# Cross-attention and self-attention in one block of instructions, with self-attention's buffers on memory that cross-attention has finished with

## The reference

```
def xattn(x, context, Wq, Wkv, null_kv, Wout, ln_scale, ln_bias):     # 16 heads of 64
    q = split_heads(x @ Wq) * 64 ** -0.5
    k, v = split(context @ Wkv)                       # a null key and value stand ahead of each
    out = softmax(q @ k.T) @ v                        # 256 x 512 for each batch and head
    return layernorm(out @ Wout) * ln_scale + ln_bias

def ffn(x, ...):                                      # 16 query heads of 8, 8 key heads
    h = rmsnorm(x) * ln1_w
    q, k, v = rope(h @ wq), rope(h @ wk), h @ wv
    x = x + softmax(causal(q @ k.T / sqrt(8))) @ v @ wo
    h = rmsnorm(x) * ln2_w
    return x + moe(h)                                 # softmax router, 2 of 8 experts

x = x + xattn(layernorm(x), ctx_2048, ...)
x = x + ffn(layernorm(x), ...)
```

## Time and profile before

| | us |
|---|---|
| median of 3 executions | 651.12 (650.49 to 651.89) |
| the profiled execution | 651.96 |
| its span, first to last instruction | 649.9 |
| busy PE, DVE, ACT, POOL in the span | 567.8, 495.3, 419.7, 322.9 |

### The profile page before, as it was taken

One profiled execution on the slowest core, in us unless ns is written; L12 is line 12 of the kernel. 1 busy time (PEld: TensorE's weight loads), 2 busy tenths in 40 slices (PEclk: granted clock), 3 DMA queues, 4 the chain that ended last, 5 costly groups with the idle time before them and its releaser, 6 DMA issues. The chain is left out here.

```text
span 649.9 us, 11036 instructions
## 1 busy us (share of the span) xinstructions
PE 567.8 (87%) x3380; PEld 444.1 (68%) x3380; DVE 495.3 (76%) x1030; ACT 419.7 (65%) x1024; POOL 322.9 (50%) x606
## 2 busy tenths in 40 slices
PE   2959999999999889999987748899986599999996
PEld 1737868777677677787766636665554578888885
DVE  4757877886889587888689625998984479999995
ACT  2538777786767657777667415898883365656653
POOL 1345766785678765787667646466965100000000
PEclk9989999999999899999989865999998599999999
DMA  7020000000100000000000002002220000000001
GB/s 263 2 59 1 2 33 2 1 2 2 32 2 2 2 1 1 1 2 2 2 0 2 2 21 73 1 3 86 85 86 2 0 1 1 1 1 1 2 0 33
DMA packets 14393, 13.14 MB, mean 20 GB/s; under 512 B 2048, under 2 KB 13696, under 8 KB 14336
## 3 DMA queue, kind: packets, MB, share of 16 engines
q1 hardware_dynamic: 14032, 12.41, 6.0%
q10 hardware_dynamic: 304, 0.03, 0.0%
HBM read 11.92 MB, written 0.52 MB: 19 GB/s over the span
## 5 line engine op out<-in xcount | busy, mean ns | idle before, releaser
L1071 POOL TENSOR_SCALAR attn_probs<-attn_probs,rinv 128x512 f32<-128x512 f32 x128 | 87.4, 695 | 29.5 <-DVE rinv L975 29.5
L848 ACT ACTIVATE attn_probs<-bank,bias 128x512 f32<-128x512 f32 x128 | 87.3, 687 | 10.0 <-DVE bias L968 10.0
L984 DVE TENSOR_TENSOR pT_lo<-bank,pT_hi 128x512 fp32r<-128x512 f32 x128 | 87.4, 685 | 7.2 <-ACT pT_hi L864 5.8
L701 PE MATMUL bank<-ident,attn_probs 128*128 128x128 f32 x512 | 77.6, 285 | 12.5 <-POOL attn_probs L1071 11.8
L960 DVE TENSOR_REDUCE neg_max<-bank 128x1 f32<-128x512 f32 x128 | 82.0, 682 | 6.7 <-PE bank L686 6.7
L864 ACT ACTIVATE pT_hi<-bank 128x512 fp32r<-128x512 f32 x128 | 73.3, 594 | 15.3 <-PE bank L701 15.0
L701 PEld LDWEIGHTS bank<-ident,attn_probs 128*128 128x128 f32 x512 | 57.4, 143 | 36.5 <-POOL attn_probs L1071 21.0
L731 PE MATMUL bank<-pT_hi,vals 128*128 128x256 f32 x256 | 67.6, 295 | 2.2 <-DVE pT_lo L984 1.4
L731 PE MATMUL bank<-pT_lo,vals 128*128 128x256 f32 x256 | 65.6, 288 | 0.0
L1885 ACT ACTIVATE act_hi<-act_f 128x512 fp32r<-128x512 f32 x56 | 35.4, 633 | 43.4 <-DVE act_f L1926 43.3
L731 PEld LDWEIGHTS bank<-pT_hi,vals 128*128 128x128 f32 x256 | 49.9, 195 | 4.3 <-issue 1.7
(11 more groups left out here) (311 smaller groups left out, 1614.5 us busy)
## 6 DMA issues: line engine op xcount, KB each, us to landing
ctx_raw<-in_ctx SPq DMA_DIRECT2D x4, 512.0 KB, 4.8
wkv_raw<-in_L_xattn_Wkv SPq DMA_DIRECT2D x2, 1024.0 KB, 10.4
gu_raw<-in_L_ffn_w_gate SPq DMA_DIRECT2D x4, 448.0 KB, 3.6
gu_raw<-in_L_ffn_w_up SPq DMA_DIRECT2D x4, 448.0 KB, 4.4
dn_raw<-in_L_ffn_w_down SPq DMA_DIRECT2D x4, 448.0 KB, 5.4
x<-in_x SPq DMA_DIRECT2D x1, 512.0 KB, 6.8
wq_raw<-in_L_xattn_Wq SPq DMA_DIRECT2D x1, 512.0 KB, 10.3
wout_raw<-in_L_xattn_Wout SPq DMA_DIRECT2D x1, 512.0 KB, 12.1
```

Source lines behind the costliest of these rows:

```text
L701: last = pe.transpose(t_bank[half][:, j * N + t * P:j * N + (t + 1) * P], probs[:, g % 2, i, t, kt * P:(kt + 1) * P], k.ident[:, :])
L848: act.activation(probs[:, g % 2, i, t, :], score_bank(G, i)[:, :], ACT.Exp, bias=bias[:, t, h:h + 1], scale=X_SCALE, accum_out=row_sum[:, ...
L984: dve.tensor_tensor(pT_lo[:, i, 2 * half:2 * half + 2, :], t_bank[half][:, :].rearrange("p (j n) -> p j n", j=2), f(pT_hi[:, i, 2 * half:2 ...
L1071: pool.tensor_scalar(probs[:, g % 2, i, t, :], probs[:, g % 2, i, t, :], rinv[:, t, h:h + 1], 1.0, ALU.mult, ALU.mult).then_inc(p_norm_s, 1)
```

## The change

Both attentions become one block, in one function `attention`, which calls `self_attention` as a supplier of pieces. The buffers of self-attention are laid over memory of cross-attention in such an order that those used first lie on what is done first (the projection weights); what cross-attention keeps to the end lies under the experts' weights. PE's banks are the same memory as before.

- Batch 0's quads are all made by POOL, ahead of its step 29; batch 1's ahead of step 32; clearing and the values of batches 0 and 1 ahead of step 33; the rest of POOL's list comes after step 34.
- PE makes the four `features` of batch 0 at the ends of steps 29 to 32; ACT copies the first two in steps 29 and 30 (with the constants in 29), DVE the others in 31 and 32.
- Self-attention's steps -3 and -2 stand at the ends of steps 32 and 33, its steps -1 and 0 at the start of step 34, ahead of the last output projection; its steps 1 and later follow step 34.
- Batch 3's steps become 1 ("y"), 6 ("h") and 8 ("qkv"); DVE takes the moments of y in step 2, the residual in 3, `make_h` in 5, the rotation in 10.

```
     S.units_done = (k_ps, NP - AHEAD), (v_ps, NP - AHEAD), (v_lo_s, NP - AHEAD)
     S.queries_done, S.scored, S.exps_done = (q_lo_s, NP), (p_exp, 4 * NP), (t_lo_s, 4 * NP)
     S.weighted = o_ps, 2 * NP
...
# PE (ACT and DVE alike, with their own steps of first_features)
+            later = S.tensor(pe)
             for s in STEPS:
+                if s == NP + 2:
+                    later.step(-1)
+                    later.step(0)
                 transpose_probs(s - 1, 1, 1)
...
                 context_unit(s, 1)
+                if NP - 3 <= s < NP + 1:
+                    later.first_features(s - NP + 3)
+                if NP <= s + 0 < NP + 2 and s > NP - 1:
+                    later.step(s - NP - 3)
+            for s in range(1, later.END):
+                later.step(s)
...
# POOL
+            later = S.gpsimd(pool)
             for s in STEPS:
+                if s == NP - 3:
+                    later.quads(0)
+                if s == NP:
+                    later.quads(1)
+                if s == NP + 1:
+                    later.first_values()
                 whole_sum(s, 1)
...
+            later.rest()
...
-        POST_STEPS = {-3: "y", 5: "h", 7: "qkv"}
+        Y_STEP, H_STEP, QKV_STEP = 1, 6, 8
+        POST_STEPS = {Y_STEP: "y", H_STEP: "h", QKV_STEP: "qkv"}
...
+            def quads(b):
+                if b == 0:
+                    for done in S.units_done:
+                        pool.wait_ge(*done)
+                query_quads(b)
+                key_quads(b)
+
+            def first_values():
+                pool.wait_ge(*S.weighted)
+                pool.memset(oT[:, :, :], 0.0).then_inc(zero_s, 1)
+                pool.memset(f(v_all[:, :, :, 2 * HD]), 1.0)
+                values(0, 2)
+
+            def rest():
+                values(2, LATE_BATCH)
+                scale_y(pool, k, LATE_BATCH)
+                quads(2)
+                scale_x1(pool, k, LATE_BATCH)
+                scale_h(pool, k, LATE_BATCH)
+                split_hT(pool, k, LATE_BATCH)
+                attention_out(0)
+                rotate_keys(pool, k, LATE_BATCH)
+                values(LATE_BATCH, B)
+                quads(3)
+                attention_out(1)
...
             def extra(s):
-                if s == -3:
+                if s == Y_STEP:
                     turn_y(pe, k, LATE_BATCH, free_bank("y", LATE_BATCH))
-                if s == 5:
+                if s == H_STEP:
                     turn_h(pe, k, LATE_BATCH, free_bank("h", LATE_BATCH))
-                if s == 7:
+                if s == QKV_STEP:
                     project_qkv(pe, k, LATE_BATCH, free_bank("qkv", LATE_BATCH))
...
-            for a in (0, 2):
-                last = act.activation(query_slot(0, a), query_heads(0), ACT.Copy, scale=F_SCALE)
```

More of the change, by code:

```diff
@@ L509, in split_hT, with attention @@
     pool.tensor_tensor(k.hT_lo[:, :], k.hT[:, :], f(k.hT_hi[:, :]), ALU.subtract).then_inc(k.hT_lo_s, 1)
-def cross_attention(nc, k, dram):
-    with ExitStack() as ctx:
+def attention(nc, k, dram, own, kept):
+    with ExitStack() as ctx, ExitStack() as stage, ExitStack() as room:
         def sb(name, shape, dt=F32):
-            return ctx.enter_context(nc.sbuf_tensor(name, shape, dt))
+            return room.enter_context(nc.sbuf_tensor(name, shape, dt))
         def sem(name):
@@ L521, in bank @@
         def bank(name):
-            return ctx.enter_context(nc.psum_tensor(name, [P, BANK], F32))
-        O_KEPT = 6
+            return room.enter_context(nc.psum_tensor(name, [P, BANK], F32))
         q_hi, q_lo = (sb(f"q_{s}", [P, 2, N], F32R) for s in ("hi", "lo"))
[L526 to L530, removed]
         probs = sb("attn_probs", [P, 2, 2, QT, M])
@@ L607, in token_tile @@
             return G // (2 * HP) * QT + G % QT
+        room.close()
+        own.close()
+        S = self_attention(nc, k, dram, ctx, stage, kept)
+        S.units_done = (k_ps, NP - AHEAD), (v_ps, NP - AHEAD), (v_lo_s, NP - AHEAD)
+        S.queries_done, S.scored, S.exps_done = (q_lo_s, NP), (p_exp, 4 * NP), (t_lo_s, 4 * NP)
+        S.weighted = o_ps, 2 * NP
+        S.unit_bank = unit_bank
         block = ctx.enter_context(nc.Block())
@@ L928, in _ @@
                 context_head(s, 1)
+                if s == NP - 3:
+                    later.constants()
+                if NP - 3 <= s < NP - 1:
+                    later.first_features(s - NP + 3)
+                if NP <= s < NP + 2:
+                    later.step(s - NP - 3)
+            for s in range(1, later.END):
+                later.step(s)
         @block.vector
@@ L1046, in _ @@
                 context_tail(s, 1)
+                if NP - 1 <= s < NP + 1:
+                    later.first_features(s - NP + 3)
+                if NP <= s < NP + 2:
+                    later.step(s - NP - 3)
+            for s in range(1, later.END):
+                later.step(s)
         @block.gpsimd
@@ L1277, in values @@
                 n = last_batch - first
-                tok = k.early if n > 1 else k.late
+                tok = k.early[:, first:last_batch, :] if last_batch < B else k.late[:, :, :]
                 raw = tok[:, :, QT * (FH + KV) * HD:].rearrange("p b (t d) -> p b t d", d=HD)
@@ L1344, in bank_read, with tensor @@
+            later = Kernel()
+            later.quads, later.first_values, later.rest = quads, first_values, rest
+            return later
+        def tensor(pe):
             def bank_read(turn):
@@ L1458, in extra, with first_features, step @@
                     tokens_first(tokens_at(s))
-            for s in STEPS:
+            def first_features(u):
+                if u == 0:
+                    pe.wait_ge(*S.queries_done)
+                else:
+                    pe.wait_ge(*((qT_s, u) if u <= 2 else (kT_s, 1)))
+                features(0, u, S.unit_bank)
+            def step(s):
                 transpose_keys0(s)
                 extra(s)
-                if s == -3:
-                    for u in range(4):
-                        features(0, u, s_bank[u])
                 transpose_keys1(s)
```

221 lines of the change are left out of this document (122 added, 99 removed).

## The result

The changed kernel took 660.65 us (median of 4, 659.75 to 663.66), the kernel before 651.02 beside it: a ratio of 1.016 (95% interval 1.0132 to 1.0187). The forecast was 658.4 and "slower", so the direction and the size came out. Part of that is luck, as the stages show: terms that were too large and too small stand against each other.

A forecast was written before the change was run, and what follows sets the result against it. No engine is full; a chain through all five sets the end. Terms 3.9 + 1.4 - 6.3 + 4.3 + 2.0 + 2.0 = +7.3 on the median 651.12 gave 658.4 us; range for 8 in 10: 649.8 to 664.0.

The forecast's parts named there:

- A: POOL, step 29: batch 0's quads stand ahead of the sum, so the triple behind it comes later; +3.9 us.
- B: PE behind the hole in step 29: the granted clock falls; +1.4 us, bounds 0 and twice that.
- C: Boundary between the attentions: self-attention's first weighted values start at 398.1 instead of 404.4; -6.3 us.
- D: Self-attention's steps 6 and 8: PE waits for a bank, 1.9 and 2.4 us; +4.3 us.
- E: DVE, steps 2 and 3: batch 3's moments of y and residual exceed the spare 0.35 per step; +2.0 us.
- first rival: Steps 1, 6 and 8: the clock falls again behind each of PE's three new waits; 662.6 us, chance 0.20.
- second rival: POOL's new work beside DVE's rotation and sums holds DVE back; 659.5 us, chance 0.04.
- F: POOL's tail, from batch 3's quads to its last output: ends later as the rotation comes a step later; +2.0 us.

The follow-up runs named there:

- mended: Changed kernel with batch 3's turns first, in steps 5 and 7, residual in step 2, scales before quads, early expert split, batch 0's quads in pieces: 648.99 us, ratio 0.998.

## Why the prediction was right, and where not

**A** held: +3.9 forecast, +3.92 measured, +3.65 to +3.96 from an idle block alone.

**B** came in kind, but it was not added to what was there. PE waited 4.66 us at the hole, and behind it ran at half clock from about 350 to 353 us; the step behind that ran at full clock. One row of PE and two windows of the changed kernel:

```profile
349.51 1.94 PE L711 MATMUL bank<-ident,attn_probs 128*128 128x128 f32 x8 [4.66 <-POOL attn_probs L1113]
```
```profile
350.00:352.00 2.00, 2.00 (x11) 2.00 (x10) 1.25 (x3) 1.11 (x3) 1.92 (x6) 0.50 0.00 0
353.50:364.00 10.50, 8.41 (x64) 6.75 (x62) 8.76 (x24) 7.60 (x23) 6.12 (x16) 1.00 0.01 2
```

From the triple of step 29 to that of 30 it took 9.69 instead of 8.91, 0.78 more (0.6 to 1.5 more in the ten profiles with a block at this place). But the slow step in the earlier trace rows, from which 1.4 was taken, is the one behind it, and its fall belonged to the profile of before: 10.28 there, 9.27 to 9.30 in all ten. So from the triple of step 29 to that of 31 the change took 18.97 and before 19.19. The forecast kept the old fall and added a new one; here one took the place of the other.

**C** has the right size, -6.3 against -6.2, in part by luck. Counted from the triple of step 31, batch 2's projection began 4.6 later than before and not 3.7, the scores of pair 2 began 0.7 later than forecast, and the way from there to the first weighted values took 10.9 instead of 11.5. Its step "batch 2's projection begins at 382.8 instead of 379.1, 3.7 later" is also not what sets the end: giving 3.9 of POOL's time back moved the first weighted values by 0.1, as PE then had a new hole and ran the output projection at half clock. That run brings in a wait of its own, so it does not show what POOL's work costs there alone; nor were the early scores run alone.

**D and E** are the terms that were too small: 6.3 forecast, 11.0 measured in one profile and 8.4 in the other (95.92 against 87.53). D's mechanism was right, but it was priced without the half clock behind the waits, and step 1's wait was counted in C; undone, all three waits together give 6.4. The half clock is the first rival's mechanism, at steps 1 and 8 and at E's wait in step 4, not at step 6, where the window stays at 1.00. How the 11.0 divides between D and E no run shows, as nothing undid E alone. E failed in the sentence "it has 0.35 spare in each of eight steps": an average over eight steps is no room in step 3. The window from 406 to 412, with the residual in it, has DVE busy in 5.83 of 6 us, and the copy that PE needs was behind the residual. The trace of before could have told it: there too DVE's step 3 has no gap, and moving `make_h` (1.01) out of it makes room for half of the 2.0.

```profile
409.53:412.93 3.40, 2.67 (x22) 1.77 (x21) 3.40 (x7) 3.24 (x8) 2.13 (x4) 1.00 0.00 0
```

The products were longer by 1.0 beside POOL's quads. That is the second rival's mechanism at a place it did not name.

**F** held: +2.0 forecast, +1.99 measured; the gap closes when POOL's list is shortened.

So the total came out near by errors that offset each other. In the two profiles D and E were too small by 4.7, B too large by 1.6, and two stretches of unchanged code ran 1.6 and 0.85 shorter after than before: +8.1 against +7.3. The other 1.5 of the 2.3 by which the forecast lies below the measured median is that the profiled execution of before was longer than its kernel's median, and that of after shorter.

## What to carry to other kernels

When work is moved into another step, look at who shares its bank in that step and who stands behind it on its engine there, not at the average room of the stage. Ask too which engine works beside it: a POOL block cost DVE nothing, 1 us or 2 us by what DVE did meanwhile. And a time saved ahead of a stretch in which PE runs at half clock can be given back there: here 3.9 us were, in a run that also left PE a new hole.

## What was not expected of the hardware

DVE's instructions whose inputs both lie in SBUF stretch beside POOL's: the residual's products 0.61 to 1.61, the rotation's 0.70 to 2.49 (0.48 in the kernel before, with POOL idle), the first of them (2.18) until POOL's subtraction of 2.08 had ended. The tails, which read a bank of PSUM, take 0.68 beside the same quads. The Trainium skill, "SBUF — State Buffer", section "SBUF: two separate sides", says that the two engines take turns at a shared pair of ports and the one that starts second is blocked; the traces agree. `make_h`, which has one tensor of SBUF and two scalars for each partition as its inputs, was stretched too: 0.59 with POOL idle in the changed kernel, 1.11 beside the quads in `mended`.

The same 55 matmuls of step 28 took 8.89 us in one profile and 10.47 in another, at granted clocks of 1.00 and 0.84, and two executions of the changed kernel differ by 2.6 in "first to last": that is more than several of the terms that were to be told apart.
